# Unit maxima split in three bfloat16 parts, turned by one bfloat16 product, and a third row of maxima in each score stack

## What is computed

```
x = layernorm(x + self_attention(x))            # softmax(Q K^T / sqrt(8)) V, no mask
x = layernorm(x + cross_attention(x, ctx, mask))# masked scores are -1e9 before the softmax
x = layernorm(x + expert(x))                    # top-1 of 8, weighted by its probability
```

## Time and profile before

| what | value |
|---|---|
| median of 3 runs | 472.44 us (471.43 to 472.73) |
| span of the profiled execution | 468.0 us, first to last instruction |
| outside the span, median less span | 4.4 us |
| PE busy | 441.4 us, 94% |
| DVE busy | 400.8 us, 86% |
| ACT busy | 359.8 us, 77% |
| POOL busy | 246.1 us, 53% |
| mean granted TensorE clock | 0.981 |

### The profile page before, as it was taken

The page is one execution under the profiler, slowest core; times in us unless marked ns, Lnnn a source line. Parts: engine busy times, 40 slices in busy tenths (PEclk is TensorE's granted clock), DMA queues, the critical chain, the costliest instruction groups (busy, mean ns, idle before and its releaser), DMA issues.

```text
span 468.0 us, 10772 instructions
## 1 busy us (share of the span) xinstructions
PE 441.4 (94%) x3885; PEld 175.9 (38%) x3887; DVE 400.8 (86%) x506; ACT 359.8 (77%) x704; POOL 246.1 (53%) x382
## 2 busy tenths in 40 slices
PE   7999989999999999899999999999999999999973
PEld 2533333333334433233344333333344334343441
DVE  5989989999899698689998999999999899962175
ACT  6328878698867777688868888888868688878843
POOL 4836878976899404222446643454438154321364
PEclk9889999999999999999999999999999899999998
DMA  5859977679760172211322345322222122111001
GB/s 131 322 125 315 278 258 251 265 245 377 260 267 14 36 125 68 67 50 39 89 73 69 114 87 106 90 61 58 81 58 69 39 59 62 50 41 40 5 12 36
DMA packets 24596, 56.07 MB, mean 120 GB/s; under 512 B 6443, under 2 KB 15929, under 8 KB 22493
## 3 DMA queue, kind: packets, MB, share of 16 engines
q0 software_dynamic: 7536, 37.91, 24.9%
q1 hardware_dynamic: 16424, 17.24, 14.2%
q10 hardware_dynamic: 580, 0.20, 0.2%
HBM read 45.60 MB, written 9.18 MB: 117 GB/s over the span
## 4 chain that ended last, share of the span: by engine, by line
PE 69%; DVE 15%; DMA 5%; POOL 4%; issue 4%; ACT 2%; ACTq 0%; DVEq 0%; POOLq 0%
PE O L1491 26%; PE ST L1727 14%; PE RT L1720 7%; PE ST L1518 7%; DVE mxs L938 7%; PE RT L1506 4%; DVE mxc L955 3%; POOL big L612 3%; DMA big<-in_mask 2%; DMA Qs<-mxr 2%; PE RT L1613 2%; PE ST L1620 1%; PE O L1469 1%; DVE mxc L956 1%; PE RT L1583 1%
## 5 line engine op out<-in xcount | busy, mean ns | idle before, releaser
L1290 ACT ACTIVATE prob<-ST 128x512 f32<-128x512 f32 x512 | 280.9, 599 | 59.1 <-PE ST L1518 27.4
L938 DVE TENSOR_REDUCE mxs<-RT 128x2 f32<-128x1024 f32 x128 | 152.8, 1222 | 12.8 <-PE RT L1506 11.7
L955 DVE TENSOR_REDUCE mxc<-RT 128x2 f32<-128x1024 f32 x128 | 152.4, 1219 | 6.6 <-PE RT L1720 6.4
L1727 PE MATMUL ST<-Qs,Kc 64*128 64x512 f32 x320 | 117.8, 451 | 0.0
L1720 PE MATMUL RT<-Kr,Qs 64*128 64x512 f32 (+1 forms) x384 | 114.1, 405 | 2.2 <-issue 2.2
L1491 PE MATMUL O<-prob,vst 128*9 128x256 f32 x1280 | 99.9, 384 | 1.7 <-ACT prob L1279 0.5
L1518 PE MATMUL ST<-Qs,Kself 64*128 64x512 f32 x256 | 96.2, 447 | 2.5 <-DMA Qs<-mxr 2.4
L684 POOL DMA_DIRECT2D Kr<-kd x96 | 47.8, 503 | 85.9 <-PE RT L1720 70.8
L1506 PE MATMUL RT<-Kself,Qs 64*128 64x512 f32 x256 | 88.7, 462 | 2.2 <-DVE Kself L915 0.9
L1491 PE MATMUL O<-prob,Vs 128*9 128x256 f32 x1024 | 80.2, 385 | 1.2 <-ACT osb L1234 0.3
L1727 PEld LDWEIGHTS ST<-Qs,Kc 64*128 64x128 f32 x320 | 50.6, 185 | 66.3 <-issue 36.6
(11 more groups left out here) (219 smaller groups left out, 326.8 us busy)
## 6 DMA issues: line engine op xcount, KB each, us to landing
big<-in_mask POOLq DMA_DIRECT2D x16, 1664.0 KB, 7.6
Kc<-kd POOLq DMA_DIRECT2D x64, 80.0 KB, 2.3
Kr<-kd POOLq DMA_DIRECT2D x64, 64.0 KB, 2.1
od_s<-osb SPq DMA_DIRECT2D x16, 128.0 KB, 2.3
kd<-Vx SPq DMA_DIRECT2D x4, 512.0 KB, 6.7
Qs<-qd_x SPq DMA_DIRECT2D x8, 256.0 KB
od_x<-osb SPq DMA_DIRECT2D x14, 128.0 KB, 1.7
Qs<-qd_s SPq DMA_DIRECT2D x12, 128.0 KB, 5.9
```

Source lines behind the costliest of these rows:

```text
L938: freed(v.tensor_reduce(mxs[:, h % 2, c2, :].rearrange("p (f t) -> p f t", f=2)[:, :, q], bank[:, :].rearrange("p (f k) -> p f k", f=2), A ...
L955: return v.tensor_reduce(o[:, :, u % 4], src, AX.X, ALU.max)
L1290: freed(nc.scalar.activation(prob[:, s % SLOTS, f * HALF:(f + 1) * HALF], bank[:, :], ACT.Exp))
L1727: mm = mmul(o[:, :], Kc[STACK[f], b * P:(b + 1) * P], Qs[STACK[f], j, :], start=True, stop=not gen, skip_group_check=True)
```

## The change

The maxima are split in three bfloat16 parts instead of a float32r part and a rest. POOL makes four instructions of it instead of two, with a wait between each. The turning product reads bfloat16 operands (24 columns of parts, a bfloat16 copy of the identity, made once on POOL), so that PE runs it as one product. The third part needs a third partition in each head's stack (rows 35 and 100, `LASTROWS`), so that `max_rows` issues a second DMA of two rows, the zeros for cross attention do too, and all waits count 32 in place of 16 (96 in place of 80). On DVE, two small sums of identity columns take a third column.

```diff
--- before.py
+++ after.py
@@ -37,6 +37,7 @@
 STACK = (slice(0, 64), slice(64, P))
 PRODUCTS = (1, 64 + 3)
 MAXROWS = slice(0, 100, 33)
+LASTROWS = slice(35, 101, 65)
 PENROWS = (34, 65)
 DIRECT = 2
 UNITS = 16
@@ -188,8 +189,10 @@
         mxs = sb("mxs", [P, 2, 2, QT])
         mxc = sb("mxc", [P, 2, 2 + NP, QT])
         finx = sb("finx", [P, QT])
-        mxh = sb("mxh", [P, 2, 2, 4], F32R)
-        mxr = sb("mxr", [16, 2, P])
+        mxl = sb("mxl", [P, 1, 2, 4])
+        mxh = sb("mxh", [P, 6, 4], BF16)
+        identb = sb("identb", [P, P], BF16)
+        mxr = sb("mxr", [24, 2, P])
         osb = sb("osb", [P, 2, 256])
         aTr, aT = sb("aTr", [P, HALF]), sb("aT", [P, HALF])
         den, rden = sb("den", [64, P]), sb("rden", [64, P])
@@ -261,7 +264,7 @@
             "q0_ready q0_hi q0_z q0_stack q_ready q_full q_high q_low q_out q_in0 q_in "
             "mask_in0 mask_in1 mask_used mask_added mask_counts flags steered pen_made pen_out pen_in "
             "ctx_in kd_out kd_more k_clean vx_ones kr0 kr1 kr2 kc0 kc1 vs0 vs1 mx_init x_bias bias_tile dve_chain "
-            "rt_ready rt_free st_ready st_free pv mx mx_part mx_split mx_turned mx_copied max_in0 max_in1 "
+            "rt_ready rt_free st_ready st_free pv mx mx_part mx_split mx_turned identb_made mx_copied max_in0 max_in1 "
             "o_copied o_in0 o_in1 o_back o_last den_in rden var std xn xq_high xq_low xq_out xq_in "
             "mkv mctx mk_hi mk_ready mk_done mv_ready mv_done mrow_ready mrow_free mcol mexp mpv rows_done cols_done "
             "grow_in grow_ready gcol_in gcol_ready passed "
@@ -339,8 +342,9 @@
             def max_rows(G):
 
                 sp.wait_ge(S("mx_copied"), G + 1)
-                load(Qs[MAXROWS, G % UNITS, :].bitcast(F32).rearrange("o (t f) -> o t f", f=P), mxr[:, G % 2, :],
-                     f"max_in{G % 2}")
+                for rows, r0, r1 in ((MAXROWS, 0, 16), (LASTROWS, 16, 24)):
+                    load(Qs[rows, G % UNITS, :].bitcast(F32).rearrange("o (t f) -> o t f", f=P), mxr[r0:r1, G % 2, :],
+                         f"max_in{G % 2}")
 
             def o_rows(G):
                 sp.wait_ge(S("o_copied"), G + 1)
@@ -382,8 +386,10 @@
                 sp.wait_ge(S("pv"), 64 * (ph + 1))
                 sp.wait_ge(S("xq_out"), 32 * (ph + 1))
                 if ph:
-                    sp.wait_ge(S("xq_in"), 80 * ph)
-                load(Qs[MAXROWS, 8 * ph:8 * ph + 8, :].bitcast(F32).rearrange("o h q -> o (h q)"), zerof[:, :], "xq_in")
+                    sp.wait_ge(S("xq_in"), 96 * ph)
+                for rows, r1 in ((MAXROWS, P), (LASTROWS, P // 2)):
+                    load(Qs[rows, 8 * ph:8 * ph + 8, :].bitcast(F32).rearrange("o h q -> o (h q)"), zerof[0:r1, :],
+                         "xq_in")
                 for k in parts:
                     load(*q_part("x", k // 2, k % 2, 8 * ph, 8 * ph + 8), "xq_in")
 
@@ -521,6 +527,8 @@
             g_.memset(wcol[:, 32:63], 0.0).then_inc(S("cst"), 1)
 
             g_.memset(Qs[:, DIRECT:8, :].bitcast(F32), 0.0).then_inc(S("q_clean"), 1)
+            pool.wait_ge(S("cst"), 1)
+            g_.tensor_copy(identb[:, :], ident[:, :]).then_inc(S("identb_made"), 1)
 
             steps = [3]
 
@@ -536,7 +544,7 @@
                     h = (m - 2) * 3 // 4
                     pool.wait_ge(S("mask_used"), m - 1)
                     if h:
-                        pool.wait_ge(S(f"max_in{h % 2}"), 16 * (h // 2 + 1))
+                        pool.wait_ge(S(f"max_in{h % 2}"), 32 * (h // 2 + 1))
                     else:
                         pool.wait_ge(S("q_in"), 16 * 4)
                 pool.dma_start(maskI[m % 2], t["mask"][q * P:(q + 1) * P, w * HALFT:(w + 1) * HALFT]) \
@@ -562,9 +570,12 @@
                 if G:
                     pool.wait_ge(S("mx_turned"), G)
                 parts = finx[:, :].rearrange("p (f t) -> p f t", f=2)
-                g_.tensor_copy(mxh[:, :, 0, :], parts).then_inc(S("mx_part"), 1)
+                high = mxh[:, 0:4, :].rearrange("p (f k) t -> p f k t", k=2)
+                step(g_.tensor_copy(high[:, :, 0, :], parts))
+                step(g_.tensor_tensor(mxl[:, 0, :, :], parts, high[:, :, 0, :], ALU.subtract))
+                g_.tensor_copy(high[:, :, 1, :], mxl[:, 0, :, :]).then_inc(S("mx_part"), 1)
                 pool.wait_ge(S("mx_part"), G + 1)
-                g_.tensor_tensor(mxh[:, :, 1, :], parts, mxh[:, :, 0, :].bitcast(F32), ALU.subtract) \
+                g_.tensor_tensor(mxh[:, 4:6, :], mxl[:, 0, :, :], high[:, :, 1, :], ALU.subtract) \
                     .then_inc(S("mx_split"), 1)
 
             def low_x_queries(ph):
@@ -881,8 +892,10 @@
                 parts = ident[:, r:r + PROD].rearrange("p (a w d) -> p a w d", a=2, w=2)
                 mark(v.tensor_reduce(rowc[:, f, 0:1], ident[:, r:r + 2 * DH], AX.X, ALU.add))
                 mark(v.tensor_reduce(rowc[:, f, 1:2], ident[:, r + 2 * DH:r + PROD], AX.X, ALU.add))
-                mark(v.tensor_tensor(rowc[:, f, 2:3], ident[:, 66 * f:66 * f + 1], ident[:, 66 * f + 33:66 * f + 34],
-                                     ALU.add))
+                last = LASTROWS.start + 65 * f
+                mark(v.scalar_tensor_tensor(out=rowc[:, f, 2:3], in0=ident[:, 66 * f:66 * f + 1],
+                                            scalar=ident[:, 66 * f + 33:66 * f + 34], in1=ident[:, last:last + 1],
+                                            op0=ALU.add, op1=ALU.add))
                 mark(v.tensor_reduce(rowc[:, f, 3:4], parts[:, :, 0, :], AX.XY, ALU.add))
                 mark(v.tensor_reduce(rowc[:, f, 4:5], parts[:, :, 1, :], AX.XY, ALU.add))
                 mark(v.tensor_copy(rowc[:, f, 5:6], ident[:, PENROWS[f]:PENROWS[f] + 1]))
@@ -1221,8 +1234,8 @@
             def max_copy(G, bank=None):
                 act.wait_ge(S("mx_turned"), G + 1)
                 if G >= 2:
-                    act.wait_ge(S(f"max_in{G % 2}"), 16 * (G // 2))
-                turned = O[0:16, 256:256 + P] if bank is None else ST[bank][0:16, 0:P]
+                    act.wait_ge(S(f"max_in{G % 2}"), 32 * (G // 2))
+                turned = O[0:24, 256:256 + P] if bank is None else ST[bank][0:24, 0:P]
                 nc.scalar.copy(mxr[:, G % 2, :], turned).then_inc(S("mx_copied"), 1)
 
             def copy_o(G):
@@ -1464,15 +1477,15 @@
 
             def turn_max(G, bank=None):
                 pe.wait_ge(S("mx_split"), G + 1)
-                rows = mxh[:, :, :, :].bitcast(F32).rearrange("p f k t -> p (f k t)")
-                if bank is None:
-                    mm = mmul(O[0:16, 256:256 + P], rows, ident[:, :], start=False, stop=False, skip_group_check=True)
-                else:
-                    mm = nc.tensor.transpose(ST[bank][0:16, 0:P], rows, ident[:, :])
+                if G == 0:
+                    pe.wait_ge(S("identb_made"), 1)
+                o = O[0:24, 256:256 + P] if bank is None else ST[bank][0:24, 0:P]
+                mm = mmul(o, mxh[:, :, :].rearrange("p k t -> p (k t)"), identb[:, :], start=bank is not None, stop=bank is not None,
+                          skip_group_check=True)
                 mm.then_inc(S("mx_turned"), 1)
 
             def have_max(G):
-                pe.wait_ge(S(f"max_in{G % 2}"), 16 * (G // 2 + 1))
+                pe.wait_ge(S(f"max_in{G % 2}"), 32 * (G // 2 + 1))
 
             def have_queries(h):
                 if h < DIRECT:
@@ -1746,7 +1759,7 @@
                     U, u = (r - SELF) // RU, (r - SELF) % RU
                     if f:
                         if u == 0 and U % 8 == 0:
-                            pe.wait_ge(S("xq_in"), 80 * (U // 8 + 1))
+                            pe.wait_ge(S("xq_in"), 96 * (U // 8 + 1))
                             pe.wait_ge(S("pen_in"), 32)
                         if gen and u == 0:
                             have_rows(pe.snap(n * U + 1))
```

## The result

The changed kernel took 475.95 us (median of 6 executions, 474.78 to 483.86) beside 472.27 us for the kernel before: 1.0105 times as long, 95% interval 1.0066 to 1.0143. The forecast was 472.8 us and "no change", with a range of 469.2 to 476.0; the time lies just inside the slower end of the range, and the ratio's interval excludes no change. The profiled execution of after is a long one, 481.67 us with a span of 479.6.

A forecast was written before the change was run, and what follows sets the result against it. PE, busy 94% and holding 69% of the chain, was taken to lead. Start 0, +2.46 us by unit 10's turn and -2.1 after gave +0.4 on the 468.0 us span; with 4.4 around it, 472.8 us, range 469.2 to 476.0.

The forecast's parts named there:

- 0 + 2.46 - 2.1 = +0.4 us: Whole span: start 0, delay by unit 10's turn +2.46 us, shorter turns after it -2.1 us.
- slower by the clock: Rival: PE idle about 2 us or more at units 3 and 10 brings half clock; 474.5 or 476 us, chance 0.10.
- the term for the second DMA under the masks: Self attention, landing of unit 9's maxima: the second DMA makes the next mask DMA 0.7 us later.
- Predicted saving 0.11 us: PE at each turn: one bfloat16 product costs 0.09 us instead of 0.20 us, bounds 0 to 0.13.
- since streaming is what shrinks: PE's turning product: reason for taking 0.09 us, near the lower end, between 0.07 and 0.20 us.
- Four instructions 0.27 us apart: POOL's split: dependent instructions 0.28 us apart, 1.0 us first to last, so 0.56 us more per split.
- PE stands at +0.56 there: Self attention, wait for unit 3's maxima: PE resumes 0.56 us later, as the mask DMA follows the longer split.
- the prediction's chain: Self attention under the masks: late splits, mask DMAs and landings add up to +2.46 us at unit 10's turn.
- the change does less than it says: Rival: the bfloat16 turning product costs what the float32 one did; +2.5 us, 474.9 us, chance 0.07.
- The marks of the prediction: Signs to check: units 9 and 10 turned 1.4 and 2.5 us later, cross units 0.11 us shorter without maxima waits.
- the bound of +4.1: Self attention before unit 10: upper bound in us, if splits 5, 6, 8 and unit 6's second DMA come through.
- chain of masks in full: Rival: under the masks nothing absorbs splits or second DMAs, 4.8 us by unit 10's turn; 475.1 us, chance 0.18.

The follow-up runs named there:

- second series: Later measurements on another chip, with the kernel before run beside them; the changed kernel, unedited, took 475.22 us there, ratio 1.0054.
- idle products at all turns: Kernel before with two bfloat16 parts, one bfloat16 turning product, and three unread bfloat16 products ahead of each turn: 478.1 us, ratio 1.0136.
- second measurement: The changed kernel measured once more without any edit: 475.22 us, ratio 1.0054 to the kernel before.
- one DMA: Changed kernel without the second maxima DMA, so the third part never reaches the stack: 474.01 us, ratio 1.0048 to the kernel before.
- split of two: Changed kernel with both DMAs but two splitting instructions on POOL, third part left zero: 474.3 us, ratio 1.0057 to the kernel before.
- six rows: Changed kernel with product rows moved so one DMA fills all six rows of maxima, nothing left out: 475.4 us, ratio 1.0020 to before.
- six rows and idle products: Changed kernel with one DMA filling six rows of maxima, plus three unread products at unit 0's turn: 475.04 us, ratio 1.0122 to before.
- longer split alone: Kernel before with two more dependent POOL instructions per split, turn and DMA as before: 473.98 us, ratio 1.0059.
- product alone: Kernel before with two bfloat16 parts turned by one bfloat16 product, third part dropped, one DMA: 472.08 us, ratio 0.9958; again 470.63 us, 0.9999.
- second DMA alone: Kernel before with a second DMA per unit into rows 35 and 100, which have no weight there: 474.97 us, ratio 1.0073.

## Why the prediction was wrong

**The sum had no term for the clock, and its largest one was too small.** The prediction put 0 + 2.46 - 2.1 = +0.4 us on the span. The step that failed first is that this sum holds the clock at nothing. It stood only as the rival "slower by the clock", with a chance of 0.10, tied to idle times of PE of about 2 us or more. What the runs showed in its place: in the second series the changed kernel had a mean clock of 0.9706 beside 0.9763, which is 2.4 us, as much as the whole difference of +2.2 us in the mean; in the first measurement its clock was 0.9655. The term that was mis-sized most is the term for the second DMA under the masks, 0.7 us, where 2.8 us were measured alone. At equal clock the changed kernel comes to -0.2 and about +0.7 us, near the +0.4 of the sum. Part of this nearness is luck, because the shares of the sum were wrong, as told below.

**Where the lower clock comes from.** Eight runs with the short product and no idle work at every turn (without the first measurement) have a mean clock of 0.9708 (90 executions, standard error 0.0006). The kernel before has 0.9768 (104), and the four runs with the float32 turn or with idle products at every turn lie between 0.974 and 0.978 (42). In each of the eight the clock is below that of before in the same series, by 0.0014 to 0.0080. The gap of 0.006 is 2.5 us. It comes with the product: the second DMA and the longer split, each alone, lengthened the waits and left the mean clock where it was. That PE's lighter load is what lowers it is supported by the idle products at all turns, which brought 0.9768 back in 6 executions, and not shown beyond that. By which rule the chip grants the clock no run here shows.

The traces, one execution each, show where it was lost. Under the masks, between 32 and 190 us, the fourteen traces hold nine stretches at half clock, of 3.4 or 6.8 us. Each begins during, or within 2 us behind, a wait of PE for maxima or a split of 1.3 to 3.7 us. Two are in after (1.72 and 2.80 us of waiting), one is in its second measurement (2.86 us), and the others are in the kernels changed with one DMA, with the split of two, with six rows (two), with six rows and idle products, and in the longer split alone. So the rival's mechanism, idle time followed by 3.4 us at half clock, was right in kind. Such idle time alone was not enough: before (1.63 us of waiting), product alone in its three traces (up to 1.89 us) and the second DMA alone (1.91 us) have no such stretch there. Eight of the nine are in kernels that have the short product as well as more POOL or DMA work, and no run parts the two. The three traces of product alone have 3.4 or 6.8 us at half clock in the tail, where before has none. From the turn of unit 31 to the end, traces without such a stretch while PE works take 48.2 to 48.4 us (six traces), those with 3.4 us of it 49.9 (two), those with 6.8 us of it 51.3 to 51.8 (six). Seven of the nine traces with the short product and no idle work at every turn have such a stretch, and one of the other five. One execution of each is too little to call that shown.

**The turn.** Predicted saving 0.11 us (bounds 0 to 0.13). The step around a turn saved 0.17 us (0.75 to 0.58), beyond the upper bound. The step "since streaming is what shrinks", by way of a quarter of a 512-column product, put 0.09 us for it; 0.03 us is left. The 56 and 81 ns of the Trainium skill, "TensorE: Matmul & The Clock Gate", section "Back-to-back issue gap", would have left an estimated 0.056 to 0.081 us, nearer, and still too much: the row shows 0.03 us. In the end the sum was not far off, since not all of it came through: the product is worth 2.8 to 3.2 us at equal clock over 31 turns, 0.10 us each, where the prediction had 3.4 us. Why the rest of the 0.17 us is lost, no run shows.

**The split.** Four instructions 0.27 us apart, 1.0 us from first to last, as said. Behind units 9 and 10 the place was right too: their turns wait 1.76 and 1.31 us for POOL. By itself the longer split moved unit 10's turn by 3.5 us in its trace, and the time by 1.4 us at equal clock. The missing link, as the trace of the longer split has it, is that behind a mask's DMA which goes out later the maxima land later, and that POOL waits for these in turn.

**The second DMA.** In cross attention it cost nothing, as predicted. Under the masks the prediction gave it 0.7 us once, at the landing of unit 9's maxima. Measured alone it costs 2.8 us at equal clock. "PE stands at +0.56 there" moved unit 3's landing by the split alone and left out that the later of two DMAs decides; units 1, 2 and 4, for whose landings PE did not wait before, had no term at all. The chain of after has five landings of maxima between 30 and 130 us (start, us, what):

```profile
37.84 6.66 DMA Qs<-mxr
...
50.93 7.63 DMA Qs<-mxr
...
76.22 6.27 DMA Qs<-mxr
...
99.41 6.16 DMA Qs<-mxr
...
120.58 7.36 DMA Qs<-mxr
```

The chain of before had such a landing once, for unit 3 (beside the 2.01 us of the earlier trace rows, during most of which, from 123.0 to 124.5, the DMA share was down to 0.44):

```profile
55.59 7.33 DMA Qs<-mxr
```

So a landing under a mask took long before the change too; what is new in after is that more of them lie on the chain, and that the DMA which decides starts 0.7 us later (unit 2's pair is issued from 50.19, the second starts at 50.93). How much of the 2.8 us is the later start, and how much the landing itself, no run parts.

Without any saving by the product the prediction's chain gives 2.7 us (2.46 with its two subtractions of 0.11 put back; its rival "the change does less than it says" has +2.5, which leaves them in). The two runs that have one part each measured 2.8 + 1.4 = 4.2 us at equal clock. So the term was too small by about a third, and its shares were wrong: two thirds of it are the DMA's, where the prediction gave the DMA about a quarter.

**The marks of the prediction.** The turns of units 9 and 10 were to be 1.4 and 2.5 us later and to wait longer for POOL: they were 12.2 and 13.0 us later in the trace of after, 5.6 and 7.0 us in that of the second measurement, where 7.0 is beyond the bound of +4.1 and only unit 9's turn waits for POOL (2.86 us). These traces hold 10.2 and 6.8 us at half clock inside the stretch of the masks, that of before none, so they mix both causes. Cross units were to be 0.11 us shorter: from the turn of unit 20 to that of unit 21 it is 12.8 us instead of 13.0, and in the two traces of the product alone the turns of units 16 to 31 gain 2.0 us on before, 0.13 each. No column product of cross attention waits for maxima, as said. That the dearer "chain of masks in full" (475.1 us) came so near the median is an accident of size: at equal clock that much is not there. The other rival near it, "the clock" with 474.5 or 476 us, is the one whose mechanism the traces bear out in part.

**What stays open.** It is open why 0.17 us less work of PE per unit goes with a lower clock, and whether a version exists that holds the clock and keeps the product's 3 us. Idle products cost more than they return at every turn, and at the start no gain of theirs was found. The version to keep is the product with two parts and one DMA. Its three measurements (two plain, one with idle products at the start) give 0.9958, 0.9999 and 0.9946: in their mean 0.3% faster. That is not clearly more than the noise: the means of all executions differ by -0.9, +0.5 and -2.4 us, with about 1 us of error each. It leaves the third part of the maxima out; with all three parts, no kernel here was faster than before.

## What to carry to other kernels

Take the mean granted clock of every execution beside its time, and compare kernels at equal clock before arguing about waits. Work taken off a PE that is busy 94% of the time can come back as a lower clock. A small DMA put beside large ones is priced by its landing under them, not by its issue. Laying the rows out so that one DMA carries all saved 1.4 us at equal clock here, but no time that could be told from noise. Compare a trace with that of a kernel which lacks only the part in question before a wait is charged to it: the wait at unit 1 was there with one DMA too. On a chain in which two queues wait for each other's landings, a step of 0.56 us can be worth several times that at one place; a kernel with that step alone tells its price, where a trace of the whole change does not.

## What the runs showed of the hardware

- Time follows the mean granted clock within one and the same kernel: 466.45 us at 0.988 to 479.64 us at 0.960 in one series, with nothing changed. The medians of before in the four series lie at 471.22 to 473.82 us.
- The same work of the tail takes 48.4 us at full clock, 49.9 us with 3.4 us at half clock in it, and 51.6 us with 6.8 us (before, after, product alone).
- A bfloat16 product of 128 columns with 24 columns of weights adds 0.03 us to PE's step between other work (293.74 to 294.32 against 294.98 to 295.53), its float32 twin 0.20 us. Three of 128 columns of weights in a row add 0.40 us.
- A DMA of 8 or 4 KB of maxima landed 6.2 to 7.8 us after its start while the masks were being read (7.8 us in the longer split alone, started at 110.52), and 1.69 us after it at 135.28 in after, where the DMA share was 0.17. Over one such landing of after (its window, columns as above) the DMA share is 1.02, and 308 GB/s were moved; in cross attention the same pair of DMAs held up no product.

```profile
50.90:58.60 7.70, 4.90 (x52) 1.65 (x48) 5.82 (x6) 4.73 (x9) 4.51 (x6) 0.98 1.02 308
```
- Dependent POOL instructions of 128x8 start 0.27 us apart, whether they write bfloat16 or float32 (a split in after, POOL's timeline):

```profile
132.97 0.18 POOL L574 CAST mxh<-finx 128x8 bf16<-128x8 f32 x1
133.23 0.20 POOL L575 TENSOR_TENSOR mxl<-finx,mxh 128x8 f32<-128x8 f32 x1
133.50 0.19 POOL L576 CAST mxh<-mxl 128x8 bf16<-128x8 f32 x1
133.77 0.20 POOL L578 TENSOR_TENSOR mxh<-mxl,mxh 128x8 bf16<-128x8 f32 x1
```
